# Three layer norms of a transformer stack turned in token halves

## The reference, cut to what matters

```python
x = x + _L0_xattn_ref(_layernorm(x), ctx, ...)   # 32 heads, rotary
x = x + _L0_ffn_ref(_layernorm(x), ...)          # silu(x w1 + b1) * (x w2 + b2), then w3
x = x + _L1_xattn_ref(_layernorm(x), ctx, ...)
x = x + _L1_ffn_ref(_layernorm(x), ...)          # dense base, and 8 experts of rank 16 under a sparsemax router
x = x + _L2_xattn_ref(_layernorm(x), ctx, ...)
x = x + _L2_ffn_ref(_layernorm(x), ...)          # router over 64 experts of rank 16, the best 16 kept
x = x + _L3_xattn_ref(_layernorm(x), ctx, ...)   # masked, heads of 16
x = x + _L3_ffn_ref(_layernorm(x), ...)          # two products of rows rounded to int8
```

## Time and profile before

| | |
|---|---|
| three runs | 1874.48, 1876.07, 1881.0 us; median 1876.07 us |
| profiled execution | 1874.18 us, span 1872.4 us, mean granted PE clock 0.978 |
| busy | PE 1749.7 us (93%), DVE 1426.5 us (76%), ACT 1048.8 us (56%), POOL 886.8 us (47%) |
| instructions | 28955 |
| DMA | 226.13 MB, mean 121 GB/s |

### The profile page before, as it was taken

How to read it: one execution, slowest core, us unless ns; L and a number is a source line. 1 busy time by engine, 2 the same in 40 slices (tenths; PEclk the granted TensorE clock), 3 DMA queues, 4 the chain that set the end, 5 groups by cost and what they waited for, 6 DMA issues and landing times.

```text
span 1872.4 us, 28955 instructions
## 1 busy us (share of the span) xinstructions
PE 1749.7 (93%) x9892; PEld 1418.2 (76%) x9892; DVE 1426.5 (76%) x3036; ACT 1048.8 (56%) x1999; POOL 886.8 (47%) x863
## 2 busy tenths in 40 slices
PE   6899999999888999979899999999989999998988
PEld 5677777787677788867788888888767778776755
DVE  6787888878777887756777778778864687777898
ACT  5766677667135565622656556556631487775333
POOL 6776776774732222053534444343347441333762
PEclk9999999999998999989999999999999999999999
DMA  5756756566418998851788878889762100120110
GB/s 183 147 105 147 139 116 143 133 114 124 116 39 162 203 202 166 154 124 47 141 172 175 157 164 187 160 172 186 148 144 88 46 19 6 51 87 29 68 46 23
DMA packets 524177, 226.13 MB, mean 121 GB/s; under 512 B 493696, under 2 KB 503168, under 8 KB 516736
## 3 DMA queue, kind: packets, MB, share of 16 engines
q1 hardware_dynamic: 524032, 224.28, 55.4%
HBM read 97.08 MB, written 5.24 MB: 55 GB/s over the span
## 4 chain that ended last, share of the span: by engine, by line
PE 59%; DVE 19%; issue 7%; ACT 5%; POOL 5%; DMA 4%; SPq 2%; POOLq 0%; DVEq 0%; ACTq 0%
PE ps_t L339 8%; PE ps_t L340 7%; PE ps_t L341 7%; PE ps_s L339 7%; PE ps_s L341 6%; PE ps_s L340 6%; PE ps_o L1900 3%; PE ps_o L339 3%; PE ps_o L340 3%; PE ps_o L341 3%; PE ps_t L1931 3%; ACT ps_s L1252 2%; PE ps_s L1886 2%; DVE l_q_lo L1002 2%; DVE nmax L1282 2%
## 5 line engine op out<-in xcount | busy, mean ns | idle before, releaser
L1252 ACT ACTIVATE ps_s<-ps_s,nmax 128x768 f32<-128x768 f32 (+1 forms) x320 | 252.4, 789 | 332.9 <-DVE nmax L1282 244.5
L1225 ACT ACTIVATE l_ab<-ps_s,rinv 128x768 f16<-128x768 f32 (+1 forms) x320 | 260.8, 815 | 73.3 <-DVE rinv L1337 59.2
L1327 DVE SCALAR_TENSOR_TENSOR l_ab<-ps_s,rinv,l_ab 128x768 f16<-128x768 f32 (+1 forms) x320 | 289.1, 903 | 1.1 <-ACT l_ab L1225 0.7
L1282 DVE TENSOR_REDUCE nmax<-ps_s 128x1 f32<-128x768 f32 x192 | 183.5, 956 | 126.6 <-PE ps_s L341 126.1
L339 PE MATMUL ps_o<-l_pt,l_v 128*128 128x256 f16 (+1 forms) x832 | 230.9, 278 | 15.1 <-DMA l_pt<-l_ab 5.5
L340 PE MATMUL ps_o<-l_pt,l_v 128*128 128x256 f16 (+1 forms) x832 | 229.5, 276 | 0.0
L341 PE MATMUL ps_o<-l_pt,l_v 128*128 128x256 f16 (+1 forms) x832 | 229.5, 276 | 0.0
L339 PE MATMUL ps_s<-l_k_hi,l_q_hi 128*128 128x512 f32 (+3 forms) x512 | 187.0, 365 | 24.1 <-DVE l_ab L1327 18.5
L377 POOL TENSOR_TENSOR wo_hi<-raw_big,one 128x512 fp32r<-128x512 f32 (+2 forms) x100 | 103.6, 1036 | 196.8 <-PE ps_t L341 120.3
L340 PE MATMUL ps_s<-l_k_lo,l_q_hi 128*128 128x512 f32 (+3 forms) x512 | 180.3, 352 | 0.0
L341 PE MATMUL ps_s<-l_k_hi,l_q_lo 128*128 128x512 f32 (+3 forms) x512 | 179.9, 351 | 0.0
(11 more groups left out here) (386 smaller groups left out, 4953.0 us busy)
## 6 DMA issues: line engine op xcount, KB each, us to landing
raw_big<-in_l_wq SPq DMA_DIRECT2D x18, 1024.0 KB, 5.8
raw_big<-in_l_wo SPq DMA_DIRECT2D x18, 1024.0 KB, 6.0
w_raw<-in_f_w SPq DMA_DIRECT2D x32, 256.0 KB, 3.6
raw_big<-in_f_w SPq DMA_DIRECT2D x7, 1024.0 KB, 4.9
raw_kv<-in_l_wkv SPq DMA_DIRECT2D x12, 512.0 KB, 6.7
l_pt<-l_ab SPq DMA_TRANSPOSE x320, 3.7
raw_f<-in_f_w SPq DMA_DIRECT2D x4, 1024.0 KB, 4.8
w_nat<-in_f_w1n SPq DMA_DIRECT2D x16, 256.0 KB, 3.8
```

The source lines that it names most:

```text
L1225: e.activation(sp.ab[:, (k - 1) % 3, 0, :], self.scores_out(k - 1), ACT.Copy, scale=rinv[:, i:i + 1]).then_inc(s_pa, 1)
L1252: e.activation(self.scores_out(k), self.scores_out(k), ACT.Exp, bias=nmax[:, i:i + 1], scale=-1.0 if l.rope else 1.0, accum_out=rsum[:, i: ...
L1282: e.tensor_reduce(nmax[:, i:i + 1], o, AX.X, ALU.max, negate=True).then_inc(s_max, 1)
L1327: e.scalar_tensor_tensor(out=b, in0=self.scores_out(t), scalar=rinv[:, i:i + 1], in1=a, op0=ALU.mult, op1=ALU.subtract).then_inc(s_pb, 1)
```

## The change

It concerns the norms 1, 3 and 5; number 7 keeps its code under a condition.

The banks now belong to half and pair of feature blocks: bank 0 holds features 0 to 255 of tokens 0 to 255, bank 1 features 256 to 511 of these tokens, banks 2 and 3 the same of tokens 256 to 511. Each has the same 512 elements a partition. `g_full` counts a bank when the odd token tile's second square of it is written, so that the two banks of half 0 are signalled after token tile 1. ACT makes the high parts by half and pair. DVE makes the low parts of half 0 between the `veps` of half 1 and the scaling of half 1, and those of half 1 after the scaling.

PE issues a first part of the block's product after the transposes of token tile 1 and ahead of those of token tile 2 (`early`): in block 0 the columns of half 0 of the first tile (12 matmuls of 256 columns in place of a part of 12 of 512), in block 1 the first 9 of the 12 matmuls of token tile 0, in block 2 the columns of half 0 of the router product. The rest of these tiles follows after all transposes. The waits for the feature blocks are now `half_turned`, by half and pair.

```diff
@@ Norm.dve
                     self.dve_stats(e, link, 1)
+                    if self.i == 7:
+                        self.dve_scale(e, 1)
+                        f3_norm_dve(e, link)
+                        return
+                    self.half_lo(e, 0)
                     self.dve_scale(e, 1)
-                    if self.i == 7:
-                        f3_norm_dve(e, link)
-                    else:
-                        turn_dve(e, self.c.g, self.c.hi, xT, self.banks)
+                    self.half_lo(e, 1)
                     return
@@ Norm
+            def half_lo(self, e, half):
+                for p in range(2):
+                    lo_dve(e, *self.half_planes(half, p)[1::-1], self.half_bank(half, p), self.c.hi + 2 * half + p)
+            def half_planes(self, half, p):
+                return [a[:, 2 * p:2 * p + 2, half * SQ:(half + 1) * SQ] for a in xT]
+            def half_bank(self, half, p):
+                return self.banks[2 * half + p].rearrange("p (d t) -> p d t", d=2)
-            def pe(self, e):
+            def pe(self, e, early=None):
+                if self.halves and self.i != 7:
+                    for t in range(TT):
+                        half = t // 2
+                        e.wait_ge(s_xn, TT * self.i + t + 1)
+                        for d in range(DK):
+                            mm = e.transpose(self.half_bank(half, d // 2)[:, d % 2, t % 2 * P:t % 2 * P + P],
+                                             xn[:, t, d * P:(d + 1) * P], ident[:, :])
+                            if t % 2 and d % 2:
+                                mm.then_inc(g_full, 1)
+                        if t == 1:
+                            early(e)
+                    return
@@ Norm.act
+                elif self.halves:
+                    for half in range(2):
+                        for p in range(2):
+                            hi_act(e, self.half_planes(half, p)[0], self.half_bank(half, p), self.c.g + 2 * half + p)
+        def half_turned(e, c, half, d):
+            e.wait_ge(g_free, c.g - 4 + 2 * half + d // 2 + 1)
@@ token_gemm(..., begun=0)
-                o = take_bank(e, n + t, c)
+                o = ring_of(n, c) if t == 0 and begun else take_bank(e, n + t, c)
                 for k in kts:
-                    if c is c1:
-                        turned(e, c, k, n + t)
+                    if t == 0 and k < begun:
+                        continue
+                    if c is c1 and n == 0 and t % 2 == 0:
+                        half_turned(e, c, t // 2, k)
@@ block 0
+        def f0_half(e, half):
+            o = ring_of(0, c0)
+            for d in range(DK):
+                half_turned(e, c0, half, d)
+                mm = passes(e, o[:, half * SQ:(half + 1) * SQ], planes(W["q"], slice(None), d, slice(0, P)),
+                            planes(xT, slice(None), d, slice(half * SQ, (half + 1) * SQ)), d == 0, d == DK - 1)
+            return mm
+        def f0_early(e):
+            e.wait_ge(w_rdy["q"], 8 * c0.q + 8)
+            take_bank(e, 0, c0)
+            f0_half(e, 0)
         def f0_pe(e):
+            f0_half(e, 1).then_inc(g_full, 1)
@@ block 1
+        def f1_early(e):
+            e.wait_ge(w_rdy["kv"], 8 * (c1.kv + 1))
+            o = take_bank(e, 0, c1)
+            for k in range(DK - 1):
+                half_turned(e, c1, 0, k)
+                passes(e, o[:, 0:256], xT_of(k, 0), planes(W["kv"], slice(None), k, slice(0, 256)), k == 0, False)
         def f1_pe(e):
-            e.wait_ge(w_rdy["kv"], 8 * (c1.kv + 1))
-            token_gemm(e, 0, c1, ..., range(DK), 256)
+            token_gemm(e, 0, c1, ..., range(DK), 256, begun=DK - 1)
@@ block 2
+        def f2_half(e, half):
+            for d in range(DK):
+                half_turned(e, c2, half, d)
+                mm = passes(e, ps_t[0][0:64, half * SQ:(half + 1) * SQ], planes(W["kv"], slice(None), d, slice(0, 64)),
+                            planes(xT, slice(None), d, slice(half * SQ, (half + 1) * SQ)), d == 0, d == DK - 1)
+            return mm
+        def f2_early(e):
+            e.wait_ge(w_rdy["kv"], 8 * (c2.kv + 1))
+            f2_half(e, 0)
         def f2_pe(e):
-            ... 12 matmuls of 512 columns into ps_t[0]
+            f2_half(e, 1).then_inc(s_f2r, 1)
@@ order of PE
-            norms[1].pe(e)
+            norms[1].pe(e, f0_early)
-            norms[3].pe(e)
+            norms[3].pe(e, f1_early)
-            norms[5].pe(e)
+            norms[5].pe(e, f2_early)
```

More of the change, by code:

```diff
@@ L1384, in take_bank, with token_gemm @@
             return ring[r]
-        def token_gemm(e, n, c, a, b, kts, width=512):
+        def token_gemm(e, n, c, a, b, kts, width=512, begun=0):
             for t in range(TT):
-                o = take_bank(e, n + t, c)
+                o = ring_of(n, c) if t == 0 and begun else take_bank(e, n + t, c)
                 for k in kts:
-                    if c is c1:
-                        turned(e, c, k, n + t)
+                    if t == 0 and k < begun:
+                        continue
+                    if c is c1 and n == 0 and t % 2 == 0:
+                        half_turned(e, c, t // 2, k)
                     mm = passes(e, o[:, 0:width], a(k, t), b(k), k == kts[0], k == kts[-1])
@@ L1452, in f0_pe @@
                     n = 2 * j + (role == "o")
+                    if n == 0:
+                        continue
                     o = take_bank(e, n, c0)
                     for d in range(DK):
-                        turned(e, c0, d, n)
                         mm = passes(e, o, planes(W[role], slice(None), d, slice(j * P, (j + 1) * P)),
@@ L1522, in program @@
         s_f1h = sem("f1_experts_weighted")
+        def f1_early(e):
[4 more added lines that the diff above has]
+                passes(e, o[:, 0:256], xT_of(k, 0), planes(W["kv"], slice(None), k, slice(0, 256)), k == 0, False)
         def f1_pe(e):
-            e.wait_ge(w_rdy["kv"], 8 * (c1.kv + 1))
-            token_gemm(e, 0, c1, xT_of, lambda k: planes(W["kv"], slice(None), k, slice(0, 256)), range(DK), 256)
+            token_gemm(e, 0, c1, xT_of, lambda k: planes(W["kv"], slice(None), k, slice(0, 256)), range(DK), 256, begun=DK - 1)
             e.wait_ge(w_rdy["q"], 8 * (c1.q + 1))
@@ L1593, in f2_pool @@
             split_all(e, "o", c2.o + 1, c2.g + 9)
-        def f2_pe(e):
[L1596 to L1602, removed]
+        def f2_half(e, half):
[7 more added lines that the diff above has]
+            f2_half(e, 0)
+        def f2_pe(e):
+            f2_half(e, 1).then_inc(s_f2r, 1)
             o = take_bank(e, 0, c2)
```

## The result

| | before | after |
|---|---|---|
| median, five runs each | 1876.07 us (1874.48 to 1881.0) | 1866.24 us (1862.9 to 1872.93) |
| ratio | | 0.995, 95% interval 0.9932 to 0.9968 |
| again, in another set | 1875.7 us (29 runs) | 1867.66 us (6 runs), ratio 0.9957, 0.9943 to 0.9972 |
| profiled execution | 1874.18 us, span 1872.4 | 1868.25 us, span 1866.5 |

What follows compares the result with a forecast made beforehand. The prediction took the kernel as one long relay of waits, TensorE carrying 59% of the chain and VectorE 19%. Gains of 1.2+3.3+1.1 = 5.6 us brought the median from 1876.07 to 1870.5 us, own range 1868 to 1873, wide 1866 to 1875.5.

Steps and rivals of the forecast that it cites:

- The stalls and the hand-over on VectorE: Three norms: TensorE stalls shrink from 3.83, 3.11, 3.83 to 3.2, 2.5, 3.2 us; low parts replace VectorE's wait for `rstd`.
- The clock comes back in the place of the stall: Three norms: with the early product filling TensorE, low-clock stretches last 3.4 us or are absent, where they lasted 6.8 to 6.9.
- I am wrong if they are still 6.8 us long: Sign of failure at the three norms: TensorE's low-clock stretches are still 6.8 us long in the profile after.
- Block 1: Norm before the second feed-forward block: last token tile earlier by 3.3 us, the middle of 2.6 and 4.0.
- Block 2: Norm before the third feed-forward block: second product, a router product, ends 1.1 us earlier with the clock back in between.
- So all three pass through: Behind the three norms: the gains of 1.2, 3.3 and 1.1 us survive to the end of their blocks.
- the other sign of being wrong: Sign of failure in the blocks: an equal wait appears further on in the block.
- case (d): Rival for the three blocks: something else ends at the same time and takes over the wait; 1876.1 us, chance 0.05.
- The weight loads: 256-column products: if loads were not hidden, 12 more in each of two places would give back 2.6 us; taken as hidden.
- Rival (a): Three norms: the clock never falls, as stalls are cut to 2.5 to 3.2 us; gain 9.4, 1866.7 us, chance 0.20.
- (b): Three norms: the clock comes back no sooner than before; gains 0.4, 1.2, 0.2, sum 1.8, 1874.3 us, chance 0.20.
- (c): Three norms: slower, second transposes queue behind slow early matmuls and the clock is held low; +1.3, 1877.4 us, chance 0.05.

Runs made afterwards that it cites:

- after_again: The changed kernel as it is, run once more against the kernel before: 1867.66 us, ratio 0.9957.
- only_block1: The kernel before with only the norm ahead of block 1 turned by halves with an early product: 1870.96 us, ratio 0.9982 against the kernel before.
- only_block2: The kernel before with only the norm ahead of block 2 turned by halves with an early product: 1874.0 us, ratio 0.9985 against the kernel before.
- clock_kept_after: The changed kernel plus 11, 8 and 11 matmuls with unused results ahead of the early products: 1866.44 us, ratio 0.9953 against the kernel before.
- splits_later: The changed kernel with POOL's split of block 0's last weight waiting for the first hidden tile's low part: 1866.24 us, ratio 0.9944 against the kernel before.

## Why the prediction was right or wrong

- **The stalls and the hand-over on VectorE: right.** 3.16, 2.44 and 3.16 us against 3.2, 2.5 and 3.2; the low parts in the place of the wait for `rstd`; stride at no cost.
- **The clock comes back in the place of the stall: right in blocks 1 and 2** (3.4 us low each, as forecast). In block 0 it failed: "I am wrong if they are still 6.8 us long" came true there. The second product ran at full speed all the same, and f_e was 0.9 us earlier (1.2 forecast), but with the help of a fall that came 2.0 us earlier than before, which was luck: in after_again the stretch was 10.2 us long, and f_e 0.3 us later than before. "The early product fills exactly that time" is borne out in a stronger form than meant: any matmuls that fill it do as well (1867.9 and 1867.6 us).
- **Block 1: the term was 0.6 too large.** 3.3 was a middle of 2.6 and 4.0, which no single execution was to show; the profiles of after and after_again show 2.7 and 2.8, that of only_block1 4.25. Both ends were priced well, and nothing in the traces chooses between them.
- **Block 2: 1.1 forecast, 1.5 found** (1.0 in only_block2).
- **Block 0: the step "So all three pass through" failed.** 1.2 us were forecast and 1.1 found at the first reciprocal of the profile of after, but 0.0 at the second: the other sign of being wrong, an equal wait further on. I had checked when the partner weights are ready, and not what POOL's later splits do to a VectorE instruction that moves against them. This is case (d) in one block: not the same end of a wait, but a VectorE instruction that takes 1.80 us in place of 0.71 beside GpSimd's. When the gain there is larger, a part gets through: with the clock held (clock_kept_after) the second reciprocal came 2.5 us earlier.
- **The sum.** 5.6 forecast; 4.1 by the local stages of the profile, 8.1 by ratio on the second set of runs. The profiled execution came to 1868.25 us against 1868.6 forecast, which was luck: 1.5 us too much in the terms and 1.8 us won where the forecast had nothing. The term that is missing is the clock elsewhere, which the sum leaves out. Over all runs the mean granted clock went from 0.978 to 0.983 in the first set and 0.981 in the second. As an estimate, (1 - mean clock) x time fell from 41.1 to 35.2 us in the second set: 5.9 us less lost to the clock in the whole kernel. The table shows one place: the last attention took 260.8 or 260.9 us in the three profiles with the old blocks 1 and 2 and no idle matmuls (13.7 us low each time), 256.2 to 258.2 in the five with the new block 1 and no idle matmuls (3.4 to 6.8 us low), and 259.3 in only_block2. That is the size of the missing 4 us. With idle matmuls it took 258.2 to 263.9, so larger local gains did not become a shorter kernel. What ties the clock in the last attention to edits ahead of it, and whether it is more than chance, is not shown: there is one profile of most kernels.
- **The weight loads.** Had they not been hidden, the prediction would have charged 2.6 us. It took the loads of both places at 128 columns, while the router's weights have 64 (`128*64` in the rows), so the charge was too large. It did not fall due: the 256-column products of block 2 start every 0.11 to 0.12 us at full clock in the profile of after (1405.13 to 1406.27 in ten steps).
- **Rival (a)** was given 1866.7 us and the time is near it, but by a different road: the clock did fall in the profile of after. **Rivals (b) and (c)** describe block 0 in after_again; for the kernel as a whole they did not decide.

## What to carry to other kernels

Where TensorE idles before a burst of products, read the granted clock behind the stall as well as the stall itself: filling it with anything may be worth as much as filling it with the right work (1867.6 and 1867.9 us against 1867.7 here), and a probe with idle matmuls prices that in one run. A gain on VectorE can be lost where its instructions that read only SBUF land on GpSimd's at their new time (f_h_lo with two inputs, f_s with one), so look at the pair of engines up to the next hand-over. And where one kernel scatters by 10 us through its clock, a part of 1 or 2 us is judged by the stage in the profile, and the whole by many runs.

## What the runs showed of the hardware that was not expected

- The first f_h_lo of block 0 took 0.70 or 0.71 us in the four profiles where it began 0.11 to 0.12 us ahead of a GpSimd piece, and 1.80 to 1.83 us in the seven where it began 0.01 to 0.03 us behind one; f_s behind it, with one input, took 1.26 inside a GpSimd piece and 0.42 where it began just ahead of one (503.73 against 503.89 in splits_later). The reciprocal took its 3.35 us in every case.
- The clock fell behind a stall of 2.44 us in one profile and not behind 2.58 us in another, of the same code at that place.
- Low clock in stages that no edit touched took 0 to 8.0 us ahead of block 0, 17.1 to 27.3 us in the second attention, 0 to 7.6 us in the third, and 3.4 to 17.1 us in the last.
